# Pairing the self-attention score passes of a decoder layer over the two row halves of the matmul array

## The reference, cut to what matters

```python
x = x + attn(layernorm(x))
x = x + xattn(layernorm(x), ctx)
x = x + ffn(layernorm(x))

# attn, per batch and head
att = q @ k.T / sqrt(8)
mask = tril(ones(256, 256), k=-1)
att = softmax(att * mask)          # masked scores are 0, not minus infinity
out = (att @ v) @ Wr + br
```

## Time and profile before

| what | value |
|---|---|
| median of three runs | 993.09 us |
| range of the runs | 992.9 to 996.3 us |
| span of the profiled execution | 997.1 us |
| mean granted TensorE clock in it | 0.980 of full |
| TensorE matmul busy | 896.1 us, 90% |
| TensorE weight load busy | 694.8 us, 70% |
| VectorE busy | 540.2 us, 54% |
| ScalarE busy | 425.3 us, 43% |
| GpSimd busy | 289.7 us, 29% |

### The profile page before, as it was taken

One profiled execution on the slowest core, in us unless ns is written; L12 is line 12 of the kernel. 1 busy time (PEld: TensorE's weight loads), 2 busy tenths in 40 slices (PEclk: granted clock), 3 DMA queues, 4 the chain that ended last, 5 costly groups with the idle time before them and its releaser, 6 DMA issues.

```text
span 997.1 us, 19846 instructions
## 1 busy us (share of the span) xinstructions
PE 896.1 (90%) x6528; PEld 694.8 (70%) x6528; DVE 540.2 (54%) x1291; ACT 425.3 (43%) x887; POOL 289.7 (29%) x495
## 2 busy tenths in 40 slices
PE   1697998998898899899899887789999999999998
PEld 0354766666676676676666666779888888888887
DVE  0443565475475465556547543556655555555554
ACT  1133555545645645555554564334222222222221
POOL 2235345435435524634633543242000000000000
PEclk9995999999999999999999999789999999999999
DMA  7124144134134224414413411000000000000000
GB/s 237 32 51 105 42 112 128 34 99 123 40 99 116 58 82 116 93 52 111 126 34 101 124 36 58 9 1 1 2 11 1 11 11 0 11 11 0 11 11 11
DMA packets 64282, 57.49 MB, mean 58 GB/s; under 512 B 5872, under 2 KB 57984, under 8 KB 64128
## 3 DMA queue, kind: packets, MB, share of 16 engines
q1 hardware_dynamic: 64256, 57.15, 21.8%
HBM read 45.20 MB, written 11.53 MB: 57 GB/s over the span
## 4 chain that ended last, share of the span: by engine, by line
PE 77%; ACT 5%; issue 5%; DVE 5%; POOL 3%; SPq 1%; DMA 1%; POOLq 0%; DVEq 0%; ACTq 0%
PE banks L194 20%; PE banks L203 13%; PE banks L653 7%; PE banks L610 7%; PE banks L588 4%; PE banks L636 4%; PE banks L590 3%; PE banks L691 3%; POOL prob L1142 3%; PE banks L581 2%; PE banks L583 2%; ACT prob L862 2%; DVE xmax L984 2%; PE banks L717 1%; PE banks L672 1%
## 5 line engine op out<-in xcount | busy, mean ns | idle before, releaser
L268 ACT ACTIVATE prob<-banks 128x512 f32<-128x512 f32 x144 | 86.0, 598 | 228.1 <-PE banks L194 178.7
L306 DVE TENSOR_TENSOR prob<-banks,prob 128x512 f32<-128x512 f32 x144 | 99.3, 691 | 107.0 <-ACT prob L268 106.9
L203 PEld LDWEIGHTS banks<-w_sb,prob 128*128 128x128 f32 x1152 | 139.1, 192 | 6.0
L203 PE MATMUL banks<-w_sb,prob 128*128 128x128 f32 x1152 | 140.4, 275 | 0.0
L194 PE MATMUL banks<-x_hi,w_hi 128*128 (+1 forms) x288 | 120.7, 419 | 0.1
L653 PE MATMUL banks<-info,xprobT 128*128 128x128 f32 (+1 forms) x832 | 108.3, 282 | 9.6 <-ACT xprobT L838 9.6
L976 DVE TENSOR_REDUCE mx<-banks 128x2 f32<-128x512 f32 x128 | 87.3, 683 | 50.8 <-PE banks L590 50.7
L194 PE MATMUL banks<-x_lo,w_hi 128*128 (+1 forms) x288 | 114.3, 397 | 0.0
L862 ACT ACTIVATE prob<-banks 128x512 f32<-128x512 f32 x192 | 99.8, 617 | 32.4 <-PE banks L676 32.4
L194 PE MATMUL banks<-x_hi,w_lo 128*128 (+1 forms) x288 | 113.6, 394 | 0.0
L653 PEld LDWEIGHTS banks<-info,xprobT 128*128 128x128 f32 (+1 forms) x832 | 100.0, 195 | 17.2 <-ACT xprobT L838 17.2
(11 more groups left out here) (143 smaller groups left out, 1388.3 us busy)
## 6 DMA issues: line engine op xcount, KB each, us to landing
infoT<-in_ctxT SPq DMA_DIRECT2D x16, 800.5 KB, 5.8
info<-in_ctx SPq DMA_DIRECT2D x16, 768.0 KB
kst<-k_stack SPq DMA_DIRECT2D x32, 192.0 KB
q_parts<-parts SPq DMA_DIRECT2D x32, 96.0 KB, 2.3
k_stack<-parts SPq DMA_DIRECT2D x32, 96.0 KB, 2.3
qst<-q_parts SPq DMA_DIRECT2D x32, 96.0 KB
w_raw<-in_w SPq DMA_DIRECT2D x16, 144.0 KB, 5.5
k_stack<-parts SPq DMA_DIRECT2D x32, 64.0 KB, 2.1
```

The source lines that it names most:

```text
L203: mm = pe.matmul(ps[:, Y_BANKS[n], t * D:(t + 1) * D], lhsT=h[n][z][:, t * P:(t + 1) * P], rhs=w2_sb[:, e, z, :], start=(z == 0), stop=(z ...
L268: act.activation(sil[z], ps[:, 2 * z, :], ACT.Silu).then_inc(s["silu_done"], 1)
L306: dve.tensor_tensor(h[n][z], ps[:, 2 * z + 1, :], sil[z], ALU.mult).then_inc(s["h_done"], 1)
```

## The change

Both passes issue the head groups of half 0 and half 1 in turn, matmul by matmul, into two banks. A pair in `alpha` covers one kind of one head group of each half: p = 0 to 5. All of its row matmuls come first, then two mask matmuls. It waits for the maxima of both units of the pair before it. `gamma(k, steps)` does the same with banks (5, 6) and (3, 4) in turn. `prob[a]` now belongs to half a, and its head groups are a's first (k = 0) and second (k = 1); `values(n)` has k = n % 2 and a = n // 2, and comes in the order 0, 2, 1, 3. The diff, cut where it only repeats the new unit numbers:

```diff
 # SyncE: reload of the stacks
-                            apart(sp, "gamma_ps", 12 * i + 6 * a + 6)
+                            apart(sp, "gamma_ps", 12 * i + 11 + a)
...
 # TensorE
-                def alpha(u0, u1):
+                def alpha(p):
...
+                    kind, local = p % 3, 4 * (p // 3)
+                    rows = (slice(0, QROWS), slice(64, 64 + QROWS))
+                    banks = (ps[:, 5, :], ps[:, 6, :])
+                    if p == 0:
+                        pe.wait_ge(s["stack0_in"], 16 * 4 * i + 16 * 4)
+                        pe.wait_ge(s["stack1_in"], 16 * 4 * i + 16 * 4)
+                        if old:
+                            pe.wait_ge(s["p_exp"], 12 * i)
+                    else:
+                        pe.wait_ge(s["alpha_max"], 12 * i + 2 * p)
+                    if kind == 0:
+                        for c in range(4):
+                            for bank, r in zip(banks, rows):
+                                pe.matmul(bank[:, c * P:(c + 1) * P], lhsT=qst[r, local + c, 0:P], rhs=kst[r, local + c, 0:P],
                                           start=(c == 0), stop=False, skip_group_check=True)
...
+                        for bank in banks:
+                            pe.matmul(bank, lhsT=ident_bf[:], rhs=mask_bf[:].rearrange("p a b -> p (a b)"),
+                                      start=False, stop=True, skip_group_check=True).then_inc(s["alpha_ps"], 1)
...
-                def gamma(n):
+                def gamma(k, steps):
...
+                    for z in steps:
+                        kind, v = KINDS[z], 6 * k + 2 * z
+                        if v == 0:
+                            pe.wait_ge(s["mrows0_in"], 48 * i + 48)
+                            pe.wait_ge(s["mrows1_in"], 48 * i + 48)
                         if v >= 4:
-                            pe.wait_ge(s["p_exp"], 12 * i + v - 3)
+                            pe.wait_ge(s["p_exp"], 12 * i + v - 2)
+                        for c in range(2 if kind < 2 else 4):
+                            for a in range(HA):
+                                r = slice(64 * a, 64 * a + KROWS)
+                                bank = KEY_BANKS[(v + a) % 4]
...
 # values(n)
-                    if n == 2:
+                    k, a = n % 2, n // 2
+                    if n == 1:
                         pe.wait_ge(s["oT_sb"], 2 * i + 1)
-                    pe.wait_ge(s["p_masked"], 12 * i + 3 * n + 3)
+                    pe.wait_ge(s["p_masked"], 12 * i + 6 * k + 5 + a)
...
-                alpha(0, 1)
                 cross_scores(0)
...
-                alpha(1, 3)
+                alpha(0)
...
-                alpha(3, 4)
+                alpha(1)
                 cross_transposes(0)
-                alpha(4, 5)
                 cross_scores(1)
...
-                alpha(5, 6)
+                alpha(2)
                 cross_values(0)
-                alpha(6, 7)
...
-                alpha(7, 8)
+                alpha(3)
                 cross_transposes(1)
-                alpha(8, 9)
...
                 cross_scores(2)
-                alpha(9, 10)
+                alpha(4)
...
-                alpha(10, 11)
                 cross_values(1)
-                alpha(11, 12)
+                alpha(5)
...
                 cross_values(3)
-                gamma(0)
-                gamma(1)
+                gamma(0, range(3))
...
+                gamma(1, (0,))
                 values(0)
-                gamma(2)
+                values(2)
+                gamma(1, (1, 2))
                 values(1)
-                gamma(3)
-                values(2)
                 values(3)
...
 # ScalarE
+                def p_exp(k, steps):
...
+                            if z == 0 and k == 1:
+                                act.wait_ge(s["pv_ps"], NG * i + a + 1)
+                            act.activation(prob[a][:, kind * 512:(kind + 1) * 512], ps[:, KEY_BANKS[v % 4], :], ACT.Exp, scale=SCALE
...
-                p_exp(0)
+                p_exp(0, (0,))
...
-                p_exp(1)
+                p_exp(0, (1, 2))
...
-                p_exp(2)
-                p_exp(3)
+                p_exp(1, range(3))
...
 # VectorE
-                alpha_max(0, 1)
...
-                alpha_max(1, 2)
+                alpha_max(0)
...
-                alpha_max(2, 3)
+                alpha_max(1)
...
-                alpha_max(3, 6)
                 cross_max(1)
+                alpha_max(2)
                 beside(-3)
-                alpha_max(6, 9)
+                alpha_max(3)
                 cross_max(2)
                 beside(-2)
-                alpha_max(9, 10)
-                alpha_max(10, 11)
+                alpha_max(4)
...
-                alpha_max(11, 12)
+                alpha_max(5)
```

More of the change, by code:

```diff
@@ new lines, in alpha @@
+                    if kind == 0:
+                        for c in range(4):
+                            for bank, r in zip(banks, rows):
+                                pe.matmul(bank[:, c * P:(c + 1) * P], lhsT=qst[r, local + c, 0:P], rhs=kst[r, local + c, 0:P],
+                                          start=(c == 0), stop=False, skip_group_check=True)
+                        for bank in banks:
+                            pe.matmul(bank, lhsT=ident_bf[:], rhs=mask_bf[:].rearrange("p a b -> p (a b)"),
+                                      start=False, stop=True, skip_group_check=True).then_inc(s["alpha_ps"], 1)
+                    else:
+                        for c in range(2):
+                            g = local + 2 * (kind - 1) + c
+                            for bank, r in zip(banks, rows):
@@ L588, in alpha @@
                                 pe.matmul(bank[:, c * S:(c + 1) * S], lhsT=qst[r, g, P:S], rhs=kst[r, g, :],
                                           start=(c == 0), stop=False, skip_group_check=True)
-                            mm = pe.matmul(bank.rearrange("p (c n) -> p c n", c=2)[:, :, P:S], lhsT=ident_bf[:],
-                                           rhs=mask_bf[:, 0:2, :], start=False, stop=True, skip_group_check=True)
-                        mm.then_inc(s["alpha_ps"], 1)
+                        for bank in banks:
+                            pe.matmul(bank.rearrange("p (c n) -> p c n", c=2)[:, :, P:S], lhsT=ident_bf[:],
+                                      rhs=mask_bf[:, 0:2, :], start=False, stop=True, skip_group_check=True
+                                      ).then_inc(s["alpha_ps"], 1)
@@ L962, in statistics, with alpha_max @@
                         dve.bn_aggr(mvt[:, t, :], stt[:, t, :]).then_inc(s[aggr], 1)
-                def alpha_max(u0, u1):
+                def alpha_max(p):
                     if not new:
                         return
-                    for u in range(u0, u1):
-                        n, kind = u // 3, u % 3
-                        dve.wait_ge(s["alpha_ps"], 12 * i + u + 1)
-                        bank = ps[:, 5 + u % 2, :]
+                    kind = p % 3
+                    for a in range(HA):
+                        n = 2 * a + p // 3
+                        dve.wait_ge(s["alpha_ps"], 12 * i + 2 * p + a + 1)
+                        bank = ps[:, 5 + a, :]
                         if kind == 0:
@@ L1132, in info_low, with masked @@
                                            ).then_inc(s["info_lo_done"], 1)
-                def masked(n):
+                def masked(k, steps):
                     if not new:
                         return
-                    for z, kind in enumerate(KINDS):
-                        apart(pool, "p_exp", 12 * i + 3 * n + z + 1)
-                        v = prob[n % 2][:, kind * 512:(kind + 1) * 512]
-                        v = v.rearrange("p (c q) -> p c q", c=2)[:, :, 0:P] if kind < 2 else v.rearrange("p (c q) -> p c q", c=4)
-                        pool.affine_select(out=v, in_=v, compare_op=ALU.is_gt, fill=0.0, base=0,
-                                           pattern=[[0, 4 if kind == 2 else 2], [1, P]], channel_multiplier=-1
-                                           ).then_inc(s["p_masked"], 1)
+                    for z in steps:
+                        kind = KINDS[z]
+                        for a in range(HA):
+                            apart(pool, "p_exp", 12 * i + 6 * k + 2 * z + a + 1)
+                            v = prob[a][:, kind * 512:(kind + 1) * 512]
+                            v = v.rearrange("p (c q) -> p c q", c=2)[:, :, 0:P] if kind < 2 else v.rearrange("p (c q) -> p c q", c=4)
+                            pool.affine_select(out=v, in_=v, compare_op=ALU.is_gt, fill=0.0, base=0,
+                                               pattern=[[0, 4 if kind == 2 else 2], [1, P]], channel_multiplier=-1
+                                               ).then_inc(s["p_masked"], 1)
                 for g in (-4, -3, -2):
@@ L1185, in step @@
                 info_low(0, slice(0, H0))
-                masked(0)
+                masked(0, (0,))
                 if crs:
```

(2 more changed lines are left out.)

71 lines of the change are left out of this document (21 added, 50 removed).

## The result

| | before | after |
|---|---|---|
| median of the runs, us | 993.0 | 1066.1 (1061.3 to 1070.9) |
| ratio, 95% interval | | 1.073 (1.069 to 1.076) |
| span of the profiled execution, us | 997.1 | 1069.1 |
| step, mean of steps 2 to 15, us | 36.0 | 40.2 (39.0 to 40.8 in the loop) |
| start of step 2, the first with all three stages (end of `q2_lo` before it), us | 95.0 | 106.1 |

The forecast was 1008 (993 to 1026). The direction was right and the size was not: +73 us instead of +15. Of the 72 us between the spans 61 lie in steps 2 to 15 and 11 ahead of them.

The account below looks back on a forecast made before the run. The prediction took TensorE to bound the step's front and a chain of hand-overs, its end set by ScalarE's exponentials, the rest. Terms summed to +0.95 us over 14 steps, plus 2 for steps 0 and 1: 1008 us, range 993 to 1026.

Parts of the forecast that it names:

- (a): Step's front: paired alpha with both halves overlapping spares TensorE time, -2.0 us per step, or -0.7 without overlap.
- (b): Front: new waits before alpha(1), the on transposes and the last pair, +1.2 us per step, bounds 0.5 and 1.7.
- (c): Behind the last alpha pair: two reductions instead of one before negm, +0.5 us per step.
- (d): Before gamma: it now waits for the row sets of both halves, +0.25 us per step.
- (e): Exponentials: the seventh and eighth wait for value products, +1.0 us per step, bounds +0.3 and +1.3.
- (f): gamma on TensorE: 1.3 us spared but worth 0, being covered by ScalarE.
- Rivals 2 and 3: Halves do not overlap, 1027 us, chance 0.13; weight loads limit first-kind pairs, +0.44 per step, 1014 us, chance 0.15.
- (g): Stack reloads behind gamma: both halves' data land before alpha(0) with 2.3 us left, counted 0.
- Rival 4: Second stack comes late: alpha(0) waits up to 0.5 us per step for half 1, 1015 us, chance 0.10.
- Steps 0 and 1: Steps without cross attention, partly at half clock: +1 to +3 us together, +2 taken.
- Rivals 1 and 5: TensorE stays the bound, kernel faster, 983 us, chance 0.12; gains and waits cancel, 993 us, chance 0.14.

Follow-up runs that it names:

- e11: The changed kernel with idle filling matmuls at the step's end and half 1's four stack reloads cut to small transfers: 1021.6 us.
- e9: The kernel before with only the first pass (alpha) paired, its pairs at the later places of e5: 986.1 us, 0.993 of before.
- e14: e9 with the single, unpaired alpha units of the kernel before put two by two into the same later places: 1005.0 us.
- e4: The changed kernel with one half's row matmuls issued before the other's in both passes; the halves still ran side by side: 1066.0 us.
- e12: The changed kernel with half 1's four stack reloads cut to small transfers and no filling matmuls: 1046.0 us.
- e3: The changed kernel with 14 idle matmuls per step that nobody reads, filling TensorE's gaps at the step's end: 1064.1 us.
- e1: The kernel before with only the first pass (alpha) and its maxima paired: 994.9 us, ratio 0.999 to 1.003.
- e2: The kernel before with only the second pass (gamma) paired, with its buffers and later stack reloads: 1080.4 us, ratio 1.079 to 1.092.
- e6: e5 with 14 idle filling matmuls per step at the step's end: 1012.0 us.
- e13: e10 with a piece of gamma issued ahead of two value products, and two filling matmuls for four there: 1007.4 us.
- e10: e7 with idle filling matmuls: four probability buffers, later alpha places and filled gaps: 1011.7 us.
- e5: The changed kernel with alpha pairs 0 to 3 later in TensorE's program, VectorE's maxima in the same order: 1030.3 us.
- e7: e5 with four probability buffers instead of two, one per head group, and no filling matmuls: 1039.9 us.

## Why the prediction was wrong, by its own steps

The segments of e11 (stack and clock taken out) against before give each term its size (its shown step is 37.3; in the mean of 37.1 is step 15 with 35.1):

| stretch | forecast | e11 less before | after less before |
|---|---|---|---|
| step's start to the mask of the last pair, (a) + (b) | -0.8 | 16.98 - 17.86 = -0.9 | 18.63 - 17.86 = +0.8 |
| to the transpose of `negm`, (c) | +0.5 | 1.88 - 1.28 = +0.6 | +0.6 |
| to `gamma`, (d) | +0.25 | 8.06 - 7.36 = +0.7 | +0.7 |
| to the query copy, (e) | +1.0 | 7.98 - 7.15 = +0.8 | 8.85 - 7.15 = +1.7 |
| to the next step, (f) | 0 | 2.39 - 2.37 = 0 | 2.99 - 2.37 = +0.6 |
| sum | +0.95 | +1.3 | +4.4 |

- **(a), right in kind and nearly in size.** The halves overlap: -1.7 where -2.0 stood (e9 against e14; its own figures, unrounded, give -1.9). Rivals 2 and 3 fall: a first-kind pair takes 0.77 from its first row matmul to the next work in e11, which is the 0.33 + 0.44 of the forecast. What the gain is worth in the changed kernel was not measured, since e4 did not take it away.
- **(b) right in kind and a third too large, (c) right.** In e11 pair 1 waits 0.30 and the `on` transposes 0.46, for 0.4 and 0.5 forecast; the third wait of 0.2 does not show. That is 0.8 for 1.2 (the forecast's items add up to 1.1), within its bounds 0.5 to 1.7. The errors of (a) and (b) cancel in the first row of the table. (c) measured 0.6.
- **(d) too small.** +0.7 for +0.25: the forecast reckoned with the time at which the last row's data moved, and TensorE is released some 0.4 later: the last data moves at 353.75 to 354.00 in e11, and `gamma` starts at 354.34.
- **(e) right in size, half right in cause.** The seventh exponential starts 4.51 after the first in e11 (359.27 less 354.76); 4.45 was forecast. But removing its buffer alone moves the wait to the ninth.
- **(f) is the first step that failed.** The forecast put the spared 1.3 us at 0, since "it is covered by ScalarE", and added: "Taken away, the cover leaves TensorE idle before 348.74." That was true in time, and the idle was seen, but it was priced at the old clock. Every duration of the sum came from rows at 1.00; nothing asked what TensorE's own gaps would do to it. The step's end and the next `cross_scores(0)` at half clock, as far as the stack wait does not hide them, are in the last column: of its +1.7, 0.9 more than in e11, the 0.6 below it, and part of the front's. With the reload out of the way the low clock costs 1.6 a step (38.7 in e12 against 37.1 in e11).
- **(g) is the second.** "2.3 us are left for the data to land" came from the issue rows alone. `alpha(0)` started 4.5 us after the last issue, with the DMA engines full (share 1.01 in 347.00:351.35) of two stacks and the context loads at once. The updates of the reload's semaphore, in the trace itself though in no view shown here, put the last one as a mean over 13 steps 4.2 us after the last issue in the changed kernel, 3.1 before the change, and 2.0 in e11 with one row a transfer. So 2.3 was too short even for the reload of before, whose consumer had more time, and the other stack in front of it adds 1.0. Rival 4 had this mechanism, but its "up to 0.5 per step" was six times too small: with the clock held the reload costs 3.0 a step (40.1 in e3 against 37.1 in e11).
- **Steps 0 and 1**: +2 forecast, +11 measured. `alpha(0)` first starts at 29.56 instead of 26.55, since it needs both stacks. The clock ahead of step 2 is lower too (76 us at the lower level for 18), but in e3 it is only 27 us and step 2 starts no sooner (106.6), so the clock is not shown to be the cause. e1 and e2, each with half of the change, start step 2 at 99.1 and 99.0, 4 us late each. With reload and gaps cured (e11) +8 remain; this was the third miss, and its cause stays open.
- **Rivals 1 and 5** fall. For rival 1 TensorE would have had to be the bound; it is the bound in the front, and only there.

So the forecast's mechanism exists, and alone it gives some 13 us more than 1008: 993 + 14 x 1.3 + 8 is 1019, beside 1021.6 measured for e11. That e6 and e13 stand at 1012 and 1007 is partly luck, since they have other places and, e13, other buffers. What took the change from there to 1066 is 45 us from two effects that were not on the list at their size, the low clock and the late stacks, and that cannot be divided between them: alone they are worth 2 and 20 or 24 and 43, by the order in which one takes them away.

Left open: how much of the 4.2 us from the last reload's issue to its completion is due to the context loads behind it (their issue was not moved); what steps 0 and 1 lose by; and what e9 would gain from the same care in steps 0 and 1.

## What to carry to other kernels

Split a change into its parts before judging it: the paired first pass with places moved so that its waits are covered wins 0.7%, and the paired second pass loses 7% (e1 against after), because it frees an engine that was not the bound there and moves the release of its operands to the end. Idle time on TensorE off the critical path is not free if it opens gaps where there were none: read the granted clock of the same stretch before and after, and price the durations behind a new gap at either level. And if curing one cause changes nothing, cure the second as well before dropping the first; here 2 and 20 us became 45.

## What the runs showed of the hardware that was not expected

- The clock fell from 1.00 to 0.50 behind quite short gaps: 0.94 and 0.98 in a stretch in which TensorE was busy 2.85 of 4.82 us. It came back only in the next front, at 350.5. The length of one gap does not tell it: a single one of 1.16, ahead of `cross_transposes` at 332.21, left the clock at 1.00 in the same step. Matmuls that nobody reads, put into these gaps, kept it at 1.00 in the whole loop (e6, e10, e11, e13), for a gain of 18 us (e5 to e6), 28 (e7 to e10) and 24 (e12 to e11).
- Row matmuls of the two halves ran side by side whether they were issued in turn or, in e4, up to four of one half first: 0.33 from a pair's first row matmul to its mask in both.
- Full DMA engines move very different amounts. Over the late reload they had a share of 1.01 at 172 GB/s; before, in a stretch in which the context loads had them, it was 1.03 at 271 GB/s:

```profile
349.00:351.00 2.00, 2.00 (x13) 1.54 (x12) 1.74 (x7) 0.00 (x0) 0.40 (x2) 1.00 1.03 271
```

By the traces' DMA records, the first of the two stretches (347.00:351.35) has 76 packets of 4096 bytes, the size of a stack's row, at 0.37 us each beside some 850 of 512 bytes at 0.05. The second has packets of 512 bytes alone, at 0.03 each.
